# Down products by tokens, quartered gate products, routing in portions, ScalarE and GpSimd for results and keys in a feed-forward, attention, feed-forward kernel

## What is computed

```python
x = x + 0.5 * ffn(layernorm(x))
x = x + attn(layernorm(x))
x = x + 0.5 * ffn(layernorm(x))

def ffn(x):                                   # 8 experts, hidden 176, top 2
    scores = sigmoid(x @ gate_w.T)
    sel = top_k(scores + expert_bias, 2)
    # for each chosen expert e, with its score s:
    h = square(relu(bf16(w_up[e] @ bf16(s * x))))
    routed = bf16(w_down[e] @ bf16(h))         # summed over the two experts
    return routed + square(relu(x @ shared_w_up.T)) @ shared_w_down.T

def attn(x):
    q = x @ Wq.T + bq
    probs = softmax(q @ memory_keys.T / sqrt(128))
    return (probs @ memory_values) @ Wo.T + bo
```

## Time and profile before

| | us |
|---|---|
| median of 3 runs | 642.77 (642.2 to 643.43) |
| the profiled execution, whole time | 644.01 |
| its span, first to last instruction | 642.2 |
| mean granted TensorE clock | 0.997 of full |
| first feed-forward | 0 to about 107 |
| attention | about 107 to 553 |
| second feed-forward | about 553 to 639.7, last store until 642.2 |

### The profile page before, as it was taken

How to read it: one execution, slowest core, us unless ns; L and a number is a source line. 1 busy time by engine, 2 the same in 40 slices (tenths; PEclk the granted TensorE clock), 3 DMA queues, 4 the chain that set the end, 5 groups by cost and what they waited for, 6 DMA issues and landing times.

```text
span 642.2 us, 9438 instructions
## 1 busy us (share of the span) xinstructions
PE 609.9 (95%) x2884; PEld 430.1 (67%) x2884; DVE 531.3 (83%) x944; ACT 456.1 (71%) x765; POOL 398.9 (62%) x443
## 2 busy tenths in 40 slices
PE   7799999799999999999999999999999998999997
PEld 4455445567677787777777777777777766645543
DVE  5889887998987978978988897897898858699885
ACT  3577787566677767778777777777776775667886
POOL 4987770564486875966867777586687786524000
PEclk9899999999999999999999999999999999999999
DMA  8011210435447365374553835727355350000000
GB/s 313 6 57 42 65 34 1 114 74 131 113 96 170 73 152 113 85 173 91 132 126 79 177 85 126 152 59 178 82 121 130 77 123 1 2 17 17 34 33 33
DMA packets 36113, 59.19 MB, mean 92 GB/s; under 512 B 9312, under 2 KB 9952, under 8 KB 35936
## 3 DMA queue, kind: packets, MB, share of 16 engines
q1 hardware_dynamic: 31808, 52.82, 34.2%
q10 hardware_dynamic: 3744, 4.73, 2.9%
q0 software_dynamic: 512, 1.05, 0.6%
HBM read 8.23 MB, written 2.10 MB: 16 GB/s over the span
## 4 chain that ended last, share of the span: by engine, by line
PE 60%; DVE 24%; issue 5%; SPq 4%; ACT 3%; POOL 2%; DMA 1%; ACTq 0%; DVEq 0%; POOLq 0%
PE banks L1425 6%; PE banks L1427 6%; PE banks L1426 6%; PE banks L1466 6%; PE banks L1468 6%; PE banks L1467 6%; DVE bank_max L1143 6%; DVE E L1138 5%; PE banks L1281 4%; SPq L356 4%; PE banks L1272 4%; PE banks L1445 4%; DVE probsT L1039 4%; PE banks L1476 2%; DVE p_lo L1131 2%
## 5 line engine op out<-in xcount | busy, mean ns | idle before, releaser
L559 POOL TENSOR_TENSOR p_lo<-probsT,p_hi 128x768 fp32r<-128x768 f32 (+1 forms) x128 | 227.0, 1777 | 120.5 <-ACT p_hi L770 119.9
L1143 DVE TENSOR_REDUCE bank_max<-banks 128x1 f32<-128x1024 f32 x128 | 155.9, 1218 | 29.8 <-PE banks L1427 29.0
L770 ACT ACTIVATE p_hi<-probsT 128x768 fp32r<-128x768 f32 (+1 forms) x128 | 104.3, 816 | 27.7 <-PE banks L1468 22.8
L1425 PE MATMUL banks<-kv_lo,q_parts 128*128 128x512 f32 x256 | 111.5, 436 | 4.6 <-ACT E L795 1.7
L1138 DVE STREAM_TRANSPOSE E<-E 128x1024 f32<-128x1024 f32 x92 | 113.5, 1234 | 0.9 <-ACT E L795 0.9
L1039 DVE SCALAR_TENSOR_TENSOR probsT<-banks,E 128x1024 bf16<-128x1024 f32 x80 | 95.3, 1217 | 21.4 <-PE banks L1272 21.3
L669 ACT ACTIVATE probsT<-probsT 128x1024 bf16<-128x1024 bf16 x96 | 92.6, 982 | 23.2 <-DVE probsT L1039 18.7
L795 ACT ACTIVATE E<-banks,neg_max 128x1024 f32<-128x1024 f32 x92 | 102.4, 1113 | 8.6 <-DVE neg_max L1149 5.6
L1466 PE MATMUL banks<-p_hi,kv_lo 128*128 128x512 f32 x256 | 107.7, 421 | 0.3 <-issue 0.3
L1467 PE MATMUL banks<-p_lo,kv_hi 128*128 128x512 f32 x256 | 102.3, 400 | 0.0
L1468 PE MATMUL banks<-p_hi,kv_hi 128*128 128x512 f32 x256 | 102.2, 399 | 0.0
(11 more groups left out here) (132 smaller groups left out, 895.6 us busy)
## 6 DMA issues: line engine op xcount, KB each, us to landing
probsT<-E SPq DMA_DIRECT2D x208, 128.0 KB, 2.4
probsT<-E SPq DMA_DIRECT2D x232, 64.0 KB, 2.0
probsT<-E ACTq DMA_DIRECT2D x72, 64.0 KB, 2.3
E<-in_keys_values SPq DMA_DIRECT2D x8, 512.0 KB, 3.6
out<-X SPq DMA_DIRECT2D x8, 256.0 KB, 2.1
X<-in_x SPq DMA_DIRECT2D x1, 1280.0 KB, 8.8
probsT<-E POOLq DMA_DIRECT2D x16, 64.0 KB, 2.3
X<-in_x SPq DMA_DIRECT2D x3, 256.0 KB, 5.2
```

The source lines that it names most:

```text
L559: pool.tensor_tensor(moved_part(p_lo, ring), moved_pair(ring // UP, ring % UP), moved_part(p_hi, ring).bitcast(fp32), ALU.subtract).then_i ...
L770: act.activation(moved_part(p_hi, ring), moved_pair(ring // UP, ring % UP), ACT.Copy).then_inc(moved_hi_done, 1)
L1143: dve.tensor_reduce(bank_max[:, i % 2, h:h + 1], score_pair(u, i, h).rearrange("p b n -> p (b n)"), AX.X, ALU.max).then_inc(bank_max_done, 1)
L1425: pe.matmul(bank, qh, kl, start=True, stop=False)
```

## The change

- Gate: gate weights, padded to 32 columns, are the stationary operand; four products of 128 token columns go to four column quarters of the array (`tile_position`). The exponentials are 128x128 instead of 128x32, and VectorE turns them back by 32x32 blocks ahead of step 0 (one operation more per routing).
- Down: each chunk is four products, tokens of `hidden` stationary (128x128), `wdown_b` moving (128 columns), into two result banks used in turn. The result stands by tokens, so B is gone; the shared down products are turned in the same way (eight products of 128 columns instead of one of 512 and two of 256).
- The result of groups 0 to 6 of each feed-forward: ScalarE copies it times 0.5 (`copy_result`), GpSimd adds it to X (`add_result`). For the last group of each, VectorE's residual reads the result bank directly after D(5).
- Routing: portions of 3, 3, 4 and 4 steps (k = 0 to 2, 3 to 5 in the even group; 6 to 9 ahead of R(1), 10 to 13 behind it in the odd group), moments after those; the last two steps go to GpSimd for the groups from 2 on, except for the routing of groups 8 and 9. GpSimd does them and the spreading ahead of its statistics.
- TW moves from ahead of D(1) to behind SD, and cw from ahead of S(3) to behind it; cw reads its bank in another order of columns.
- The second feed-forward's statistics from its fifth group on are joined on GpSimd.
- ScalarE rounds keys and values, between SS and ex; GpSimd keeps `kv_lo`.

```diff
 def joins_on_pool(n):
-    return AHEAD < n <= ATTENTION_LN
+    return AHEAD < n <= ATTENTION_LN or n > SECOND_LN + AHEAD
...
+            def add_result(G):
+
+                pool.wait_ge(result_copied, added_before(G + 1))
+                xg = X[:, tiles_of(G % GROUPS), :].rearrange("p t d -> p (t d)")
+                pool.tensor_tensor(xg, xg, half_result, ALU.add).then_inc(x_added, 1)
...
                     if f == 0:
 
                         pool.wait_ge(kv_loaded[i % 2], (i // 2 + 1) * 16)
-                        pool.tensor_copy(kv_hi[:, i, :], kv_stage[:, i % 2, :]).then_inc(kv_hi_done, 1)
                         pool.wait_ge(kv_hi_done, i + 1)
...
                     shared_square(G)
+                    if f == 0:
+                        act.wait_ge(kv_loaded[i % 2], (i // 2 + 1) * 16)
+                        act.activation(kv_hi[:, i, :], kv_stage[:, i % 2, :], ACT.Copy).then_inc(kv_hi_done, 1)
...
                 if k == 0:
+                    dve.wait_ge(expz_done, G + (2 if T > GT else 1))
+                    wait(dve, route_step, STEPS * (event - 1) + 1)
...
+                        dve.transpose(turned, expz_rows[:, slots, :].rearrange("p s n -> p (s n)")
+                                      ).then_inc(expz_turned, 1)
...
+            def gate_products(bank, xt):
+
+                for t in range(GT):
+                    last = pe.matmul(bank[t * SQ:(t + 1) * SQ, :], gate_s[:, :], xt[:, t * P:(t + 1) * P], start=True,
+                                     stop=True, tile_position=(0, t * SQ))
+                last.then_inc(logits_done, 1)
...
                 for c in chunks:
-                    last = pe.matmul(y_bank[:, :], wdown_b[:, c, :], hidden[:, k, c % 2, :], start=(c == 0),
-                                     stop=(c == CH - 1))
+                    for t in range(GT):
+                        last = pe.matmul(result_banks[G % 2][:, t * D:(t + 1) * D],
+                                         hidden[:, k, c % 2, t * P:(t + 1) * P], wdown_b[:, c, :],
+                                         start=(c == 0 and t == 0), stop=(c == CH - 1 and t == GT - 1))
...
             def residual(G, g):
 
-                dve.wait_ge(z_done, G + 1)
+                dve.wait_ge(down_done, (G + 1) * SLOTS)
```

More of the change, by code:

```diff
@@ L76, in moments_before, with added_on_pool, added_before @@
     return sum(not joins_on_pool(k) for k in range(n))
+def added_on_pool(G):
+    return G % GROUPS != GROUPS - 1
+def added_before(G):
+    return sum(added_on_pool(k) for k in range(G))
 ATTENTION_LN = GROUPS
@@ L286, in routed_slots, with finishes_on_pool, routing @@
             return slice(0, 2) if G >= 2 else slice(G, G + 1)
+        def finishes_on_pool(G):
+            return G >= 2 and route_event(G) != route_event(GROUPS)
+        def routing(G):
+            T = GT * (2 if G >= 2 else 1)
+            return tuple(route[:, a, 0:T, :] for a in range(6))
         def wide_weights(G):
@@ L447, in join_halves @@
             def join_halves(n):
-                step = POOL_STEPS * (n - AHEAD - 1)
+                step = POOL_STEPS * sum(joins_on_pool(k) for k in range(n))
                 means = stats[:, :, :].rearrange("p t (a b) -> p t a b", b=3)[:, :, :, 1]
@@ L976, in route_group @@
                 T = (slots.stop - slots.start) * GT
-                score, biased, hit, tagged, first, second = (route[:, a, 0:T, :] for a in range(6))
+                score, biased, hit, tagged, first, second = routing(G)
                 top, first_tag, top2, second_tag = (best[:, a, 0:T] for a in range(4))
@@ L1086, in ffn @@
                     if i % 2 == 0 and i + 2 < GROUPS:
[L1087 removed]
+                        for k in range(0, 3):
                             route_group(k, G + 2)
@@ L1221, in gate @@
                 wait(pe, weighted, (G - AHEAD) * SLOTS)
-                for t in range(GT):
-                    last = pe.matmul(gate_bank[:, t * E:(t + 1) * E], xT[G % RING][:, t * P:(t + 1) * P], gate_s[:, :],
-                                     start=True, stop=True)
-                last.then_inc(logits_done, 1)
+                gate_products(gate_bank[:, 0:P], xT[G % RING])
             def shared_up_product(G):
@@ L1245, in transpose_weights @@
                 last.then_inc(wbc_done, 1)
-            def transpose_back(G):
-                pe.wait_ge(yT_copied, G + 1)
-                wait(pe, x_updated, G)
-                for t in range(GT):
-                    last = pe.transpose(z_bank[:, t * D:(t + 1) * D], yT[:, t * P:(t + 1) * P], ident[:, :])
-                last.then_inc(z_done, 1)
             def up(G, k):
@@ L1482, in early_gate @@
                 pe.wait_ge(xT_copied, SECOND_LN + i + 1)
-                for t in range(GT):
-                    last = pe.matmul(early_logits(i)[:, t * E:(t + 1) * E], xT[i][:, t * P:(t + 1) * P], gate_s[:, :],
-                                     start=True, stop=True)
-                last.then_inc(logits_done, 1)
+                gate_products(early_logits(i), xT[i])
             ffn(0)
```

151 lines of the change are left out of this document (93 added, 58 removed).

## The result

The changed kernel took **648.39 us** (median of 4 runs, 648.02 to 650.04) against 643.1 of the kernel before in the same comparison: **1.0077 times the time, 95% interval 1.0053 to 1.0101**. It is slower where I forecast 639.9 and faster, and the time lies above the range that I gave. The profiled execution is the slowest of the four (650.04).

What follows compares the result with a forecast made beforehand. TensorE was taken to bound even groups, VectorE odd ones. Start -2.0, first groups +1.6, seam -1.0, entry +0.3, second feed-forward -0.5, tail -1.3 sum to -2.9, off the 642.8 median: 639.9 us, range 635.5 to 647.

Steps and rivals of the forecast that it cites:

- the sentence on GpSimd: GpSimd saves 1.04 of rounding, gets the 1.27 addition and two 0.25 steps every second group; about 9.5 a group, hidden.
- the slower one: Rival: down products are paced by more than columns; 646.2 at 0.081 each, about 655 at 0.117; chance 0.2.
- Down products: TensorE's 44 products of 128 columns a group: 0.056 each, 2.46 a group, between bounds 0.054 and 0.117.
- The gate: TensorE's gate in four column quarters: 0.45 instead of 0.94, between 0.22 and 0.94, saving 0.5.
- First to second SR: Start of first feed-forward: without TensorE's 1.54 wait at TW, group 1's SR comes at 33.5 instead of 35.5, -2.0.
- Groups of the first feed-forward: Groups 1 to 7: group 1 +1.05, pair 2, 3 unchanged, pair 4, 5 +0.5, group 6 9.45; together +1.6.
- The rival that made ScalarE the bound: First feed-forward: ScalarE's rounding, 0.95, is paid in the four odd groups too, +3.8, giving 643.7; chance 0.12.
- Seam: From first feed-forward to attention: VectorE's 1.08 wait for B before the residual goes, -1.0.
- the 0.3 of the entry: Entry to the second feed-forward: two more transposes in the routing, faster gates giving some back; +0.3, between 0 and 0.6.
- Second feed-forward: Even groups 10.0, odd 11.4; first groups -0.2, two pairs -0.6, last groups +0.3; together -0.5.
- The portions' rival: Second feed-forward runs at 10.0 for five groups, 9.4 for two, 69 instead of 73.9; 635 total; chance 0.18.
- Tail: End of kernel: the last residual starts where C did, no longer waiting for B; -1.34.

Runs made afterwards that it cites:

- run 5: Changed kernel; GpSimd waits for its own addition (group 0: normalising) before the four subtractions, leaving a short gap; 642.7 us, ratio 0.9977.
- run 4: Changed kernel with the rounding of keys and values (`kv_hi`) back on GpSimd, ahead of the subtractions; 640.9 us, ratio 0.9960.
- run 10: Kernel of run 9 with TW and cw of even groups but group 0 back ahead of D(1) and S(3); 638.4 us, ratio 0.9897.
- run 12: Kernel before the change, with only the rounding of keys and values moved to ScalarE, between SS and ex; 650.3 us, ratio 1.0076.
- run 9: Kernel of run 4 with every residual on VectorE (no ScalarE copy, no GpSimd addition), each store waiting for its own group; 639.0 us, ratio 0.9909.
- run 8: Kernel of run 4 with routing portions and statistics where they stood before the change, last two steps still on GpSimd; 647.2 us, ratio 1.0055.
- runs 3: Changed kernel with GpSimd's addition behind the four `kv_lo` subtractions instead of ahead of them; 649.6 us, ratio 1.0102.
- 11: Kernel of run 10 with TW back in odd groups too, undoing the whole move of TW; 646.8 us, ratio 1.0040.
- run 1: Changed kernel; in the first feed-forward GpSimd fills `kv_lo` with zeros in four writes instead of subtracting; 644.7 us, ratio 1.0024.

## Why the prediction was wrong, point by point

By starts of SR, all in us of the profiled executions:

| stretch | before | forecast | after | run 5 |
|---|---|---|---|---|
| to the first SR | 18.3 | 18.3 | 18.8 | 18.8 |
| first to second | 17.2 | 15.2 | 17.5 | 15.9 |
| second to eighth | 64.9 | 66.5 | 72.1 | 67.8 |
| to the second feed-forward's first | 454.3 | 453.6 | 454.1 | 453.3 |
| first to last there | 74.4 | 73.9 | 74.3 | 74.3 |
| to the end | 13.0 | 11.7 | 11.4 | 11.3 |
| span | 642.2 | 639.3 | 648.2 | 641.4 |

**The step that failed** is the sentence on GpSimd: it "saves 1.04 and gets the addition", its sum stays near 9.5 a group, hidden. The sum was right (36.3 us busy in groups 2 to 5, 9.1 a group), but that does not make it hidden: VectorE's routing steps wait for GpSimd without any semaphore. I counted GpSimd by busy time and looked for waits only where the code has them. 5.9 of the 8.9 us between forecast and span are the three long steps (SR intervals of after less run 5). The sign stood in my own rows: the routing's first step lasts 1.22 in the earlier trace rows, where its median in that trace is 0.31: it asks 0.12 us after a GpSimd instruction starts (L559, 534.55 to 535.84) and ends 0.05 behind its end. I read that row for TensorE's idle time. None of my rivals had this mechanism; the slower one rested on the down products.

**Down products:** right. A pair of chunks takes 0.45, 0.056 a product, as taken; the upper end of 0.117 is far off. The chain of the changed kernel (an odd group's second half):

```profile
581.75 0.45 PE banks L1351 x8
582.20 0.43 PE banks L1336 x2
582.63 0.45 PE banks L1351 x8
583.08 0.91 PE banks L1302 x2
```

The Trainium skill's 81 ns for a stream of loads and products of this width, named in the prediction, is not what this stream does. The gate was taken at 0.45 and takes 0.36:

```profile
587.61 0.36 PE banks L1288 x8
```

**First to second SR:** forecast 15.2; with the gap it is 15.9, with the rounding on GpSimd 14.9 (run 4). The direction was right, and the 2.88 us step undid it. What the forecast didn't name is the clock: in the kernel before, TensorE's granted clock is 0.87, 0.50 and 0.78 in 26 to 28, 28 to 30 and 30 to 32 us, behind its wait of 1.54, and 1.00 there in the changed kernel and in run 5. So part of what this interval gains is clock, and not the wait itself. The first SR itself lies between 18.4 and 18.8 in the runs on the changed kernel, against 18.3 before, taken as unchanged.

**Groups of the first feed-forward:** without the long steps 67.8 against my 66.5. In run 5 group 1 is 11.4 as forecast, the pair 2 and 3 is 22.7 (forecast 22.4), 4 and 5 is 23.8 (23.2), group 6 is 9.93 (9.45). Two steps of 0.8 are left in each even group with routing; in group 4 SR follows ScalarE's last square, which waits 0.99 for R(5) behind them, so they are at least part of what makes its even groups 11.4 and not 11.0. The last interval is 9.93 since TW lies on the loop (9.49 when it is moved back, run 10). The rival that made ScalarE the bound held in part: the rounding alone costs time in the kernel before (run 12), and in run 4, without it, the intervals are 0.1 to 1.0 shorter than in run 5, but for the last, which is equal, and for groups 2 and 3 with the stretch at half clock. The times of runs 4 and 5 can't be told apart by their ratios.

**Seam:** the residual after the first feed-forward comes 11.8 behind the last SR instead of 12.7, 0.9 where I had 1.0. It stands not behind the second block of scores but behind VectorE's maximum of it:

```profile
118.85 1.23 DVE L1211 TENSOR_REDUCE bank_max<-banks 128x1 f32<-128x1024 f32 x1 [0.69 <-PE banks L1496]
...
120.18 0.68 DVE L1110 SCALAR_TENSOR_TENSOR X<-banks,X 128x512 f32<-128x512 f32 x1
```

The rest of that stretch is the attention, which differs by up to 2 us from run to run (452.6 to 454.7 for the stretch), so the 0.3 of the entry can't be judged.

**Second feed-forward:** odd groups 11.37, forecast 11.4. Even groups were forecast at 10.0 and are 10.3 and 10.2 (groups 10 and 12): the chain goes over VectorE there, where one step waits for GpSimd's addition.

```profile
589.68 0.45 DVE probs L1062
...
590.22 0.90 DVE route L1070
```

Without the addition and its copy they are 9.95 (run 9). It is the same mechanism in small. The last two intervals are 0.24 and 0.54 longer than before, where I had 0.3 for both; the first two are together 0.6 shorter, where I had 0.2. The transpose itself was 0.45, taken at 0.42. **The portions' rival** (10.0 for five groups) didn't come; portions pay 1.2 us there (run 8), and TW's move in the even groups costs 0.5 (run 10 against 9).

**Tail:** 1.6 less, forecast 1.34; the last residual now follows D(5):

```profile
645.03 0.69 DVE L1110 SCALAR_TENSOR_TENSOR X<-banks,X 128x512 f32<-128x512 f32 x1 [1.74 <-PE banks L1351]
```

**A reading:** U(4) of the odd group starts at 594.09 in the earlier trace rows and not at about 593.9; R(0) to U(4) is then 7.0 and U(4) to SR 5.15, with the same sum.

The parts, then: GpSimd's addition with its copy, and ScalarE's rounding with the row that it leaves on GpSimd, cost more than they give; undoing both gives run 9. The portions pay, with TW late in odd groups. Results by tokens and the gate weren't undone one by one: their instructions take what was forecast, and B's time at seam and end is gone.

## What to carry to other kernels

Before work goes to GpSimd, read in the trace how long VectorE's small instructions last beside it: one that lasts longer than its median at the same shape and ends within 0.1 us behind the end of a GpSimd instruction was here waiting for GpSimd, and moving GpSimd's work by a microsecond can turn 0.2 into 3.5. If GpSimd must run several instructions in a row beside such steps, a wait on its own last result ahead of the row may be all it takes. And an engine that is idle a third of the time can still have a due time: ask for each operation given to it who waits for its end, and how long before that it ends now.

## What the runs showed that I had not expected

A VectorE step with two operands in SBUF (and L1068, L1070 and L1007 with one) that asks while GpSimd works is served at the end of the GpSimd instruction or after a whole row, and this makes the difference. Served at the next end (0.04 to 0.1 us behind it): all steps that asked inside the subtractions (before, runs 3, 4, 5, 8, 9, 11, 12: 0.38 to 0.80), and those in an addition that a cast follows (run 4: 0.79). Held off for the row: those that asked during the instruction ahead of the subtractions or fills when no gap followed (2.88, 3.50, 3.51; run 1: 2.36 and 2.35, past an addition and four fills). A gap of 0.08 us is enough (run 5).

But a gap isn't always needed. In the changed kernel itself, in the routing of groups 8 and 9, the same step L1044 asks inside an addition of the same size and gets in at its end, though GpSimd's next instruction follows at once (VectorE, then GpSimd):

```profile
545.49 0.57 DVE L1044 TENSOR_TENSOR route<-route,best 128x64 f32<-128x64 f32 x1
```

```profile
544.72 1.27 POOL L629 TENSOR_TENSOR X<-X,attended 128x512 f32<-128x512 f32 x1
545.94 0.20 POOL L511 TENSOR_TENSOR neg_mean<-moments,minus_one 128x4 f32<-128x4 f32 x1
```

So that the wait is for GpSimd and that a gap ends it is shown; that the missing gap alone causes it is not: here and in run 4 there was none, and the step got in. What differs there, GpSimd's next instruction among other things, was not tried apart. By what rule that instruction goes first in the one case and not in the other stays open, as the subtractions follow each other without a gap and let in a step that asks inside them. No run was made on that.
